# Both heads' products for the next row maxima at the tail of a score unit, instead of one at its head and one at its tail

## What is computed

```python
q = (x @ Wq + bq).reshape(b, lq, H, D)          # H = 16 heads, D = 64
k = (embeds @ Wk + bk).reshape(b, lk, H, D)     # lk = 1601
v = (embeds @ Wv + bv).reshape(b, lk, H, D)
scores = jnp.einsum('bqhd,bkhd->bhqk', q, k) * SCALE
attn = jax.nn.softmax(scores, axis=-1)
ctx = jnp.einsum('bhqk,bkhd->bqhd', attn, v).reshape(b, lq, AD)
return ctx @ Wo + bo
```

## Time and profile before

| | |
|---|---|
| median of 3 runs | 2675.04 us (2674.38 to 2675.89) |
| the profiled execution's own time | 2674.98 us |
| its span in the trace | 2673.2 us |
| PE busy | 2628.4 us, 98% of the span |
| POOL busy | 2223.5 us, 83% |
| DVE busy | 2122.6 us, 79% |
| ACT busy | 1741.3 us, 65% |
| shift products L1671, all 1792 | 551.5 us busy |
| maxima products L1662, all 2048 | 572.6 us busy |
| exponentials L976, all 1536 | 834.0 us busy |

### The profile page before, as it was taken

One profiled execution on the slowest core, in us unless ns is written; L12 is line 12 of the kernel. 1 busy time (PEld: TensorE's weight loads), 2 busy tenths in 40 slices (PEclk: granted clock), 3 DMA queues, 4 the chain that ended last, 5 costly groups with the idle time before them and its releaser, 6 DMA issues.

```text
span 2673.2 us, 67748 instructions
## 1 busy us (share of the span) xinstructions
PE 2628.4 (98%) x26773; PEld 2261.2 (85%) x26773; DVE 2122.6 (79%) x4221; ACT 1741.3 (65%) x3507; POOL 2223.5 (83%) x1826
## 2 busy tenths in 40 slices
PE   6999999999999999999999999999999999999997
PEld 5888888888888888888888888888888888888875
DVE  7778888887788887888878787888778888787764
ACT  4676676666666666766766667666666667676642
POOL 2888888888888888888888888888888888888855
PEclk8999999999999999999999999999999999999998
DMA  4000100001000000000000010000100000000031
GB/s 104 16 14 8 27 9 18 16 11 25 10 17 17 18 19 12 19 12 21 16 15 16 10 28 10 15 19 11 25 10 17 16 14 16 11 9 11 7 97 36
DMA packets 154862, 53.25 MB, mean 20 GB/s; under 512 B 112049, under 2 KB 152236, under 8 KB 154545
## 3 DMA queue, kind: packets, MB, share of 16 engines
q1 hardware_dynamic: 149376, 45.28, 7.4%
q0 software_dynamic: 2048, 3.64, 0.4%
q10 hardware_dynamic: 3120, 0.01, 0.1%
HBM read 40.76 MB, written 8.72 MB: 19 GB/s over the span
## 4 chain that ended last, share of the span: by engine, by line
PE 96%; DVE 1%; POOL 1%; issue 1%; DMA 0%; ACT 0%; SPq 0%; POOLq 0%; DVEq 0%; ACTq 0%
PE ps L1707 26%; PE ps L1675 22%; PE ps L1671 10%; PE ps L1662 5%; PE ps L1653 5%; PE ps L1654 4%; PE ps L1655 4%; PE ps L1631 4%; PE ps L1633 4%; PE ps L1632 4%; PE ps L1723 3%; PE ps L1747 2%; PE ps L1606 1%; PE ps L1882 1%; PE ps L1642 1%
## 5 line engine op out<-in xcount | busy, mean ns | idle before, releaser
L748 POOL TENSOR_TENSOR key_sums<-key_sums,prob_T 65x512 f32<-65x512 f32 x1398 | 1814.9, 1298 | 160.5 <-POOL key_sums L748 2.7
L1234 DVE TENSOR_REDUCE mx<-ps 128x1 f32<-128x400 f32 (+1 forms) x2048 | 1057.6, 569 | 233.5 <-PE ps L1662 193.1
L976 ACT ACTIVATE prob_T<-ps 128x512 f32<-128x512 f32 x1536 | 834.0, 596 | 82.6 <-PE ps L1675 55.6
L1707 PE MATMUL ps<-prob_T,v_sb 128*64 128x256 f32 (+1 forms) x6656 | 740.5, 379 | 0.8 <-ACT prob_T L976 0.8
L1675 PE MATMUL ps<-q_hi,k_hi 64*128 64x256 f32 (+1 forms) x3328 | 727.7, 277 | 0.0
L1675 PE MATMUL ps<-q_lo,k_hi 64*128 64x256 f32 (+1 forms) x3328 | 727.2, 277 | 0.0
L1675 PE MATMUL ps<-q_hi,k_lo 64*128 64x256 f32 (+1 forms) x3328 | 725.9, 277 | 0.0
L1707 PEld LDWEIGHTS ps<-prob_T,v_sb 128*64 128x64 f32 (+1 forms) x6656 | 478.2, 137 | 241.5 <-ACT prob_T L976 1.7
L1675 PEld LDWEIGHTS ps<-q_hi,k_hi 64*128 64x128 f32 (+1 forms) x3328 | 576.2, 180 | 1.8 <-ACT prob_T L976 1.3
L1662 PE MATMUL ps<-k_hi,q_hi 64*128 64x400 f32 (+1 forms) x2048 | 572.6, 350 | 1.2 <-DVE q_lo L1225 1.2
L1675 PEld LDWEIGHTS ps<-q_lo,k_hi 64*128 64x128 f32 (+1 forms) x3328 | 553.5, 180 | 0.1
(11 more groups left out here) (241 smaller groups left out, 3642.9 us busy)
## 6 DMA issues: line engine op xcount, KB each, us to landing
shift_f<-row_shifts SPq DMA_DIRECT2D x256, 64.0 KB, 2.6
ctx_raw<-in_ctx_dram SPq DMA_DIRECT2D x120, 100.0 KB
row_shifts<-nm_T SPq DMA_DIRECT2D x512, 0.5 KB
prob_T<-in_L_ffn_W_dram SPq DMA_DIRECT2D x12, 256.0 KB, 5.2
slots_in<-no_row SPq DMA_DIRECT2D x1, 2080.0 KB, 15.1
x_in<-in_x_dram SPq DMA_DIRECT2D x8, 256.0 KB, 3.0
out_dram<-x1s SPq DMA_DIRECT2D x16, 128.0 KB, 1.9
v_sb<-slots_in SPq DMA_DIRECT2D x6, 260.0 KB, 3.1
```

The source lines that it names most:

```text
L748: op = nc.gpsimd.tensor_tensor(acc[0:rows, :, :], acc[0:rows, :, :], prob_T[0:rows, :, k, :], ALU.add)
L976: nc.scalar.activation(prob_T[:, h, 2 * i - 2:2 * i, :].rearrange("p k t -> p (k t)"), ps[:, bank, :], ACT.Exp).then_inc(ring_act, 1)
L1234: v.tensor_reduce(mx[:, qt, h, c:c + 1], ps[:, at.bank("mx", r, c, qt, h), 0:WID[c]], AX.X, ALU.max).then_inc(ring_dve, 1)
L1707: last = mm(ps[h * DH:h * DH + DH, bank, 0:T], v_sb[0:rows, r % NJ // 2 % 2, k, v0 + h * DH:v0 + h * DH + DH], prob_T[0:rows, h, k, :], st ...
```

## The change

The h1 product for the maxima moves from the head of a unit (behind S00) to its tail, behind S16. A unit is now issued as S00, S01, S10, S02, S11, S03, S12, S04, S13, S05, S14, S06, S15, M0, S16, M1, and the eighth unit as M0, M1. The ring's order of places changes with it, from S0, M1, S1, M0 to S0, S1, M0, M1, and so does the order in which DVE reduces a unit: h0 before h1. No product, no reduction and no transfer is added or removed.

```diff
@@ all_fills
     for unit in MAX_UNITS:
+        maximum(0, unit, 0)
         maximum(0, unit, 1)
-        maximum(0, unit, 0)
...
             for i, unit in enumerate(MAX_UNITS):
-                if i < UNITS:
-                    put("act", "s", r, i, 0)
-                if following:
-                    maximum(r + 1, unit, 1)
-                if i < UNITS:
-                    put("act", "s", r, i, 1)
+                for h in range(2 if i < UNITS else 0):
+                    put("act", "s", r, i, h)
                 if following:
                     maximum(r + 1, unit, 0)
+                    maximum(r + 1, unit, 1)
@@ maxima, row_shift
-                    for h in (1, 0):
+                    for h in (0, 1):
                         dve.wait_ge(rows_full[h], at.full("mx", r, c, qt, h))
...
-                _, count = at.freed("mx", r, 3, qt, 0)
+                _, count = at.freed("mx", r, 3, qt, 1)
@@ score_unit
                     if at_step == 0:
-                        if unit:
-                            maximum(at, s + 1, *unit, 1)
                         second = bank_of(at, "s", s, i, 1)
                     else:
                         score_step(s, 1, second, *steps[at_step - 1])
...
                 if unit:
                     maximum(at, s + 1, *unit, 0)
                 score_step(s, 1, second, *steps[-1]).then_inc(rows_full[1], 1)
+                if unit:
+                    maximum(at, s + 1, *unit, 1)
@@ batch, and the start
+                            maximum(at, s + 1, *unit, 0)
                             maximum(at, s + 1, *unit, 1)
-                            maximum(at, s + 1, *unit, 0)
```

More of the change, by code:

```diff
@@ L1841, in _ @@
             for unit in MAX_UNITS:
+                maximum(at, 0, *unit, 0)
                 maximum(at, 0, *unit, 1)
-                maximum(at, 0, *unit, 0)
             for c in range(4):
```

## The result

| | before | after |
|---|---|---|
| median | 2675.47 us (4 runs, 2674.38 to 2676.55) | 2695.69 us (4 runs, 2694.64 to 2697.36) |
| ratio, with 95% interval | | 1.0075 [1.0063, 1.0087] |
| span of the profiled execution | 2673.2 us | 2692.8 us |
| 127 score stages with maxima, mean of one | 7.803 us | 7.953 us |

The change makes the kernel 0.75% slower, 20.2 us; the forecast was 2694.6 us, 19.6 slower.

What follows compares the result with a forecast made beforehand. The prediction took PE's two halves, both full, as the bound, with S10 waiting for ACT's exponential. 127 stages x 0.15 = 19.1 us plus 0.5 for the last slot made 19.6, so 2694.6 us, range 2682 to 2710.

Steps and rivals of the forecast that it cites:

- halves as two queues: On PE, an instruction whose half is free passes those waiting for the other half, so issue order costs h0 nothing.
- much slower rival: Matmuls keep the stream's order: a unit takes 1.18 us for 1.13, 0.42 a stage, 2728 us; chance 6%.
- Step 1: From unit 3, S10 waits for the h1 exponential until S00 + 0.21; the h1 half idles once, about 0.21 us.
- Steps 2 and 3: Stage end: a second maxima product behind S16 adds 0.18 us; an earlier S10 in the last unit credits 0.03.
- Step 4: A lag of the h1 half isn't made good within the stage; example slot at 58.35: 7.88 us against 7.79.
- the lag is absorbed: Rival: the h1 half catches up within the stage, time within 2 us of 2675; chance 7%.
- Step 5: DVE's last reduction comes 0.5 to 0.57 us later; hidden in ordinary slots, 0.5 us exposed once in the last slot.
- faster rival: S10's bank is free in time and the halves run level: 0.06 us less a stage, 2667 us; chance 7%.

Runs made afterwards that it cites:

- bound_all: Changed kernel, banks dealt anew from the first score stage, but score banks from unit 2 on kept to those of two units back: 2694.39 us.
- free_all: Changed kernel, banks dealt by estimated earliest free from the first score stage on, S10 and M0 swapping banks of two units back: 2669.95 us.
- bound_last4: bound_all with M1 at the head in units 0 to 2 and at the tail in units 3 to 6: 2696.51 us.
- tail_first3: Changed kernel with M1 at the tail in units 0 to 2 only, at the head in units 3 to 6, old bank relations: 2703.95 us.
- tail_last4: Changed kernel with M1 at the head in units 0 to 2, at the tail in units 3 to 6, old bank relations: 2704.72 us.

## Why the prediction was right, point by point

**The halves as two queues** held. S00 of unit 5 starts at 1016.69, ahead of the M1 at 1016.72 that stands in front of it in the stream. The unit takes 1.11 us, not the 1.18 of the much slower rival. The trace disagrees again with the strict order of matmuls that the Trainium skill has in "TensorE: Matmul & The Clock Gate", Part 3.

**Step 1, the gap,** was right in cause and size: 0.2 us, in unit 3, with the load 0.05 to 0.06 behind the exponential's end. The swap of one pair of banks (bound_all and free_all) takes the gap away and puts it back. What I had wrong is what its row looks like. I expected S10 at S00 + 0.21 from unit 3 on; in unit 3 it is listed at + 0.09, with its bare load inside.

**Steps 2 and 3, one maxima product more at the end (0.18) less a credit (0.03),** summed to 0.15 a stage; measured 7.953 - 7.803 = 0.150, and 19.0 us over the 127 stages. The credit was chosen from one unit's row, between 0 and 0.04; over all stages S10 of the last unit comes 0.242 us behind S00 before and 0.215 after, in the mean, which is 0.03. Where it comes from, the prediction didn't say. By the starts, the h1 half is late before the change from M1's bare load at the head of unit 0 on; after it, S10 comes as early as the wait lets it. bound_all and bound_last4 measured 0.146 and 0.152 for the whole term in the same way.

**Step 4** holds: the lag wasn't made good in any of the kernels with the bound bank. Its own example was misread. M1 "starts with S00" in the stage of the earlier trace rows in its listed start only; what counts is S10, here in the slot that begins at 58.35:

```profile
58.35 0.30 PE L1671 MATMUL ps<-shift,shift_w 64*65 64x256 f32 x1
...
58.74 0.27 PE L1671 MATMUL ps<-shift,shift_w 64*65 64x256 f32 x1
```

That is 0.39 behind S00, against 0.29 (1003.91 and 1003.62 above). The h1 half was later by 0.09 to 0.10 and not by 0.13, and the stage was longer by 0.09. So nothing was made good there, and the rival "the lag is absorbed", which had 0.09 left of 0.13, had not even these 0.04 for it.

**Step 5 was half right.** The reductions do come later, and PE's wait for the shift in the last slot went from 0.97 us to 1.47 (PE; the wait is in brackets):

```profile
2586.22 0.33 PE L1668 MATMUL ps<-shift,shift_w 64*65 64x256 f32 x2 [1.47 <-ACT shift L944]
```

But the 0.5 us didn't reach the end. Part of it is the stage's own lengthening, counted twice: behind the stage's end the last S00 comes at 8.01 us, before at 7.70, so 0.31. That is regained before the first products of the last projection, which begin 22.62 us behind the end of that stage where it was 22.66. From the last stage to the end it is 114.63 us after and 114.69 before. I had named no next wait behind the late S00, and there is one: that projection waits for DVE's normalised heads (0.5 us before, 0.2 after):

```profile
PE ps L1730 <- DVE heads_T L1271: 0.2, 1, 0.2
```

So the 0.5 belongs out of the sum. The span grew by 19.0 in the stages, -0.4 between them, -0.1 behind them, and 1.1 before the first, which begins at 59.5 us and not at 58.4. That last part I can't lay to the change, as such starts differed by up to 2.5 us between kernels with that setup. That forecast and median agree to 1.1 us owes this much to luck: a term of 0.5 that isn't there stands against a later start of 1.1 that wasn't forecast; the term that carries the result is the 0.15.

**The faster rival** was judged rightly for this change: its condition, a bank of S10 free in time, isn't met. free_all meets it, and there it gives what it said: I had priced it at 0.06 a stage, and it measures 7.803 - 7.752 = 0.05.

**What I had not weighed** is the wait of the maxima themselves for DVE. In this change it stays harmless, as step 5 had it, but tail_first3 and tail_last4 show that the ring has little left there either: there the maxima product does wait for its bank, with a reduction that ends 0.05 us before its load.

## What to carry to other kernels

A product that looks misplaced at the head of a unit can be the filler of a wait: before moving it, look for the wait that follows it in the stream, the time at which that wait is released, and what the engine would do until then. Read the two halves of a row-tiled array as two queues with one sequencer: their own order sets the time, and a semaphore wait stops both (here the loads of S01 and S10, at 1014.55 and 1014.56). A late half costs once, at the next product that needs both, and it pays to ask which bank the waiting product takes; here giving S10 the bank of M0, which comes free earlier, together with M1 at the tail turned a loss of 20 us into a gain of 5.

## What the runs showed of the hardware that was not expected

A product whose weights aren't loaded ahead is listed as starting with its load, not when it streams: S10 at 1014.56 is listed level with its load, and its follower comes 0.34 us later in place of 0.23. Such a start must not be read as the end of the wait for the array; the distance to the next start in the same half shows the rest. The first M1 of a stage in the kernel before is another such row (0.28 to its follower in place of 0.18), and it hid that the h1 half begins nearly every stage late.
